# One ones matmul for two key blocks, whose exponentials GpSimd adds in place, in the attention stage of a three-stage kernel

## The reference

```
q, k, v = (heads(query), heads(key), heads(value))          # 16 heads, width 32
scores = jnp.einsum('bhqd,bhkd->bhqk', q, k)                 # 1024 x 1024, causal
at  = jax.nn.softmax(where(causal, scores, -inf) / sqrt(32), axis=-1)
out = jnp.einsum('bhqk,bhkd->bhqd', at, v) ... @ w_o + b_o
```

## Time and profile before

| | |
|---|---|
| median of 3 runs | 1262.74 us (1262.4 to 1263.25) |
| profiled execution | 1264.52 us, span 1262.7 us |
| busy, share of the span | PE 87%, DVE 72%, ACT 63%, POOL 29% |
| granted TensorE clock, mean | 0.956 |
| `core(0)` | about 457 to 626 us |
| out-projection, `project(1)` | about 626 to 658 us, 658 to 720 us |
| `core(1)` | about 722 to 894 us |

### The profile page before, as it was taken

How to read it: one execution, slowest core, us unless ns; L and a number is a source line. 1 busy time by engine, 2 the same in 40 slices (tenths; PEclk the granted TensorE clock), 3 DMA queues, 4 the chain that set the end, 5 groups by cost and what they waited for, 6 DMA issues and landing times. The chain is left out here.

```text
span 1262.7 us, 18129 instructions
## 1 busy us (share of the span) xinstructions
PE 1100.0 (87%) x5990; PEld 493.5 (39%) x5990; DVE 908.0 (72%) x2247; ACT 793.0 (63%) x1181; POOL 367.1 (29%) x400
## 2 busy tenths in 40 slices
PE   0777999987869789999999799999799799998886
PEld 0333555544434323232344233322244355554443
DVE  5788788988943787885334887783236888888793
ACT  5468798887623536667614356567235888988762
POOL 2101144444562144100220450002100124443356
PEclk9998899998998889999999899999899999999899
DMA  9200000000010222110000321110000000000000
GB/s 369 82 1 1 2 1 1 2 1 1 1 47 9 51 59 52 48 39 2 1 21 6 77 53 43 35 35 2 1 1 1 1 1 18 18 18 18 18 18 34
DMA packets 22286, 37.44 MB, mean 30 GB/s; under 512 B 5398, under 2 KB 7833, under 8 KB 21532
## 3 DMA queue, kind: packets, MB, share of 16 engines
q1 hardware_dynamic: 21404, 34.54, 8.6%
q0 software_dynamic: 768, 1.57, 0.5%
HBM read 19.17 MB, written 4.21 MB: 19 GB/s over the span
## 5 line engine op out<-in xcount | busy, mean ns | idle before, releaser
L802 ACT ACTIVATE arena<-arena,X 128x2048 int8<-128x2048 f32 x148 | 296.0, 2007 | 8.8 <-DVE X L1228 8.6
L857 ACT ACTIVATE arena<-zP,asc 128x512 f32<-128x512 f32 (+3 forms) x384 | 200.6, 582 | 109.3 <-PE zP L652 78.7
L502 PE MATMUL zP<-T,arena 128*128 128x512 f16 x1024 | 251.7, 390 | 6.7 <-DVE arena L1187 6.7
L554 PE MATMUL oP<-T,arena 128*128 128x512 f16 x832 | 206.2, 393 | 7.5 <-DVE arena L1343 7.5
L758 ACT ACTIVATE arena<-zP,sc 128x512 f32<-128x512 f32 x128 | 87.9, 689 | 107.7 <-PE zP L507 107.7
L502 PEld LDWEIGHTS zP<-T,arena 128*128 128x128 f16 x1024 | 102.5, 101 | 133.4 <-issue 16.7
L554 PEld LDWEIGHTS oP<-T,arena 128*128 128x128 f16 x832 | 83.2, 100 | 89.1 <-issue 18.7
L648 PE MATMUL zP<-arena 98*128 98x512 f16 (+3 forms) x384 | 110.6, 334 | 2.9 <-DMA arena<-arena 1.9
L1468 DVE RECIPROCAL arena<-arena 128x128 f32<-128x128 f32 x64 | 57.1, 927 | 61.7 <-ACT arena L870 61.7
L629 PE MATMUL hP<-arena 96*128 96x512 f16 (+3 forms) x256 | 84.4, 352 | 15.8 <-DVE mx L1446 12.9
L973 POOL TENSOR_SCALAR ln<-ln 128x1 f32<-128x1 f32 x32 | 38.6, 1206 | 202.5 <-DVE ln L1172 202.3
(11 more groups left out here) (196 smaller groups left out, 1876.1 us busy)
## 6 DMA issues: line engine op xcount, KB each, us to landing
arena<-arena SPq DMA_DIRECT2D x168, 64.0 KB, 2.0
arena<-in_w_synT SPq DMA_DIRECT2D x4, 1024.0 KB, 8.2
arena<-in_w_outT SPq DMA_DIRECT2D x4, 1024.0 KB, 14.8
out_dram<-x_sb SPq DMA_DIRECT2D x16, 256.0 KB, 2.0
x_sb<-in_x SPq DMA_DIRECT2D x3, 1024.0 KB, 14.0
arena<-in_w_o SPq DMA_DIRECT2D x2, 1024.0 KB, 5.0
arena<-arena POOLq DMA_DIRECT2D x24, 64.0 KB, 1.9
arena<-in_b_syn SPq DMA_DIRECT2D x1, 1024.0 KB, 11.9
```

Of the source, the lines that this page charges most:

```text
L502: pe.matmul(zP[:, c * CW:(c + 1) * CW], part[:, g % 2, k, :], T1[:, k, c * CW:(c + 1) * CW], start=(n == 0 and k == 0), stop=False)
L554: mm = pe.matmul(o, part[:, k, :], T2[:, k, :], start=(c == 0 and n == 0 and k == 0), stop=False)
L802: act.activation(junk[:, counted[0] % 2, :], Z[:, g % ZR, :], ACT.Sign, bias=X[:, 2, k:k + 1], accum_out=S[:, k:k + 1]).then_inc(sm["cnt"], 1)
L857: act.activation(PT[:, m // 4 % 2, h, q0:512], colP[m % 3][:, q0:512], ACT.Exp, scale=asc[:, g, 10:11]).then_inc(sm["exp_done"], 1)
```

## The change

In the pair of an odd key block kb and the even one before it, GpSimd adds the odd block's exponentials onto the even one's in memory, and PE then does one ones matmul for both, as wide as the even block. The product with v still reads each block. So:

- `core_order`: the ones matmul of blocks (kb-2, kb-3) stands at the end of step kb = 3, 5, 7, and that of a unit's last pair at the end of step 0 of the next unit. 48 ones matmuls of four heads in a batch become 24.
- Four buffers in place of two: `w_in` itself, the two of `PT`, and a part of `qk_mem` (from group 2 on, a part of `parts_mem`). ACT waits for the pair that used the buffer before.
- As `w_in` is overwritten, SP loads it again for batch 1, after the barrier and ahead of `w_lat`, and `project(1)` waits for it.
- POOL walks through the order too: `add_pair` at the last `col` of each odd block, the multiply and bias add of a unit at its last `rec`, and with each of the first four of these two tiles of the `bo` add.

The line numbers of the changed file are higher than before: ones matmul L693, `mix_v` L681, `col` L668 and L672, rows L649, turn L655, pair add L1059, multiply and bias add L1093 and L1094, `bo` add L1068, `w_in` loads L442.

```
             if last:
                 step.insert(len(step) - MIX_LAG, ("mix_v", *last))
-                step.append(("mix", *last))
+                if kb == 0:
+                    step.append(("mix", *last))
+                elif kb % 2 and kb >= 3:
+                    step.append(("mix", g, qc, kb - 2))
...
+        BLOCKS = [as_block(w_in.rearrange("p k n -> p (k n)")), PT[:, 0, :, :], PT[:, 1, :, :],
+                  as_block(qk_mem[:, 2048:4096]), as_block(parts_mem[:, HALF:HALF + 2048])]
+        def pt_of(g, kb):
+            return BLOCKS[4 if g >= 2 and kb % 4 == 3 else kb % 4]
...
             for b in range(2):
+                if b:
+                    eng.wait_ge(sm["mix_done"], b * TOTAL["mix"])
+                    load_w_in()
                 for k, w in ((0, w_ku), (1, w_qu), (2, w_qr), (3, w_vu)):
...
             def project(b):
-                pe.wait_ge(sm["aw_in"], 16 * 3 * KD)
+                pe.wait_ge(sm["aw_in"], 16 * 3 * KD * (b + 1))
...
+                    elif kind == "mix":
+                        qc, kb = e[2:]
+                        pe.wait_ge(sm["pair_set"], m + 1)
+                        if kb == 1 and n["norm"]:
                             pe.wait_ge(sm["sum_out"], n["norm"])
-                        q0 = max(0, kb * P - qc * 512)
+                        q0 = max(0, (kb - 1) * P - qc * 512)
                         for h in range(HG):
+                            mm = pe.matmul(sumP[h * HD:(h + 1) * HD, q0:512], ones32, pt_of(g, kb - 1)[:, h, q0:512],
+                                           start=(kb == 1), stop=(kb == 4 * qc + 3),
                                            tile_position=(0, h * HD), skip_group_check=True)
...
-                        if m // 4 >= 2:
-                            act.wait_ge(sm["mix_done"], m // 4 - 1)
+                        if m // 4 >= 4:
+                            act.wait_ge(sm["mix_done"], m // 8 - 1)
...
+                def add_pair(g, qc, kb, col):
+                    even, odd = pt_of(g, kb - 1), pt_of(g, kb)
+                    q0 = max(0, kb * P - qc * 512)
+                    pool.wait_ge(sm["exp_done"], col + 1)
+                    pool.wait_ge(sm["mv_done"], col // 4)
+                    pool.tensor_tensor(even[:, :, q0:512], even[:, :, q0:512], odd[:, :, q0:512], ALU.add)\
+                        .then_inc(sm["pair_set"], 1)
+                    pool.wait_ge(sm["pair_set"], col // 8 + 1)
...
+                for e in ORDER:
...
+                    if kind == "col" and e[3] % 2 and e[4] == HG - 1:
+                        add_pair(g, *e[2:4], m)
+                    elif kind == "norm" and m % TOTAL["norm"] == 0:
                         wait_stack(pool, b, 0)
                         wait_stack(pool, b, 1)
+                        units(2)
+                    elif kind == "rec" and e[3] == 3:
...
+                        pool.wait_ge(sm["mix_out"], b * TOTAL["norm"] + u + 1)
+                        pool.wait_ge(sm["rec_set"], m + 1)
+                        link(pool.tensor_tensor(a, a, rec_of(u), ALU.mult))
+                        pool.tensor_scalar(a, a, bcols[:, 10 + g:11 + g], None, ALU.add).then_inc(sm["attn_set"], 1)
+                        if u < 4:
+                            add_bo(range(2 * u, 2 * u + 2))
```

More of the change, by code:

```diff
@@ L263, in program @@
                  "h_set hT_ps hT_hi hT_lo mm2 out_ps y_set stats2 rstd2 yn_set x_new out_done "
[L264 removed]
+                 "consts2 mv_done pair_set bsyn_in hT_sub hT_lo2 ch_dve ch_act ch_pool phase "
                  "aw_in al_in ab_in a_stats a_rstd a_xn a_turn a_xT p_ps p_out p_max q_max q_scale split_hi split_lo wo_in bo_in "
@@ L424, in _, with load_w_in @@
                 eng.dma_start(brow[0:3, first:first + j * P], b_rows[:, first:first + j * P]).then_inc(sm["orow_in" if n else "brow_in"], 16)
+            def load_w_in():
+                for k in range(KD):
+                    for w, lo in ((w_kv, 0), (w_q, 128), (w_kr, 256)):
+                        eng.dma_start(w_in[:, k, lo:lo + w.shape[1]], w[k * P:(k + 1) * P, :]).then_inc(sm["aw_in"], 16)
             eng.wait_ge(sm["hT_ps"], 4 * NT)
-            for k in range(KD):
-                for w, lo in ((w_kv, 0), (w_q, 128), (w_kr, 256)):
-                    eng.dma_start(w_in[:, k, lo:lo + w.shape[1]], w[k * P:(k + 1) * P, :]).then_inc(sm["aw_in"], 16)
+            load_w_in()
             barrier(eng, 1)
             for b in range(2):
+                if b:
+                    eng.wait_ge(sm["mix_done"], b * TOTAL["mix"])
+                    load_w_in()
                 for k, w in ((0, w_ku), (1, w_qu), (2, w_qr), (3, w_vu)):
@@ L1018, in core, with units @@
             def core(b):
-                for g in range(3):
-                    if g == 1:
-                        load_stack(pool, b, 1, 1)
-                    elif g == 2:
+                def units(g):
+                    pool.memset(stacks[g][3 * HD:3 * HD + 2, 1, :, :], MUNIT).then_inc(sm["unit_set"], 1)
+                    pool.wait_ge(sm["unit_set"], 3 * b + g + 1)
+                def add_pair(g, qc, kb, col):
+                    even, odd = pt_of(g, kb - 1), pt_of(g, kb)
+                    q0 = max(0, kb * P - qc * 512)
+                    pool.wait_ge(sm["exp_done"], col + 1)
[3 more added lines that the diff above has]
+                    pool.wait_ge(sm["pair_set"], col // 8 + 1)
@@ new lines, in add_bo @@
+                def add_bo(tiles):
+                    pool.wait_ge(sm["bo_in"], 16 * (b + 1))
+                    pool.wait_ge(sm["a_xn"], (b + 1) * BT)
+                    for i in tiles:
+                        t = x_sb[:, b * BT + i, :]
+                        pool.tensor_tensor(t, t, bo, ALU.add).then_inc(sm["bo_added"], 1)
+                units(0)
+                load_stack(pool, b, 1, 1)
+                units(1)
+                n = {k: b * v for k, v in TOTAL.items()}
+                for e in ORDER:
+                    kind, g = e[:2]
+                    m = n[kind]
+                    n[kind] += 1
+                    if kind == "col" and e[3] % 2 and e[4] == HG - 1:
+                        add_pair(g, *e[2:4], m)
+                    elif kind == "norm" and m % TOTAL["norm"] == 0:
@@ L1024, in core @@
                         wait_stack(pool, b, 0)
                         wait_stack(pool, b, 1)
-                    pool.memset(stacks[g][3 * HD:3 * HD + 2, 1, :, :], MUNIT).then_inc(sm["unit_set"], 1)
-                    pool.wait_ge(sm["unit_set"], 3 * b + g + 1)
-                pool.wait_ge(sm["bo_in"], 16 * (b + 1))
-                pool.wait_ge(sm["a_xn"], (b + 1) * BT)
-                for i in range(BT):
-                    t = x_sb[:, b * BT + i, :]
-                    pool.tensor_tensor(t, t, bo, ALU.add).then_inc(sm["bo_added"], 1)
@@ L1033, in core @@
-                for m in range(TOTAL["norm"]):
-                    if b == 0 and m == TOTAL["norm"] - 1:
-                        rstd_rows(1, range(2))
-                    g, qc = m // 2, m % 2
-                    a = attT[:, g, qc * 512:(qc + 1) * 512]
-                    pool.wait_ge(sm["mix_out"], b * TOTAL["norm"] + m + 1)
-                    pool.wait_ge(sm["rec_set"], 4 * (b * TOTAL["norm"] + m + 1))
-                    link(pool.tensor_tensor(a, a, rec_of(m), ALU.mult))
-                    pool.tensor_scalar(a, a, bcols[:, 10 + g:11 + g], None, ALU.add).then_inc(sm["attn_set"], 1)
+                        units(2)
+                    elif kind == "rec" and e[3] == 3:
+                        u = m // 4 % TOTAL["norm"]
+                        if b == 0 and u == TOTAL["norm"] - 1:
+                            rstd_rows(1, range(2))
+                        qc = u % 2
+                        a = attT[:, g, qc * 512:(qc + 1) * 512]
+                        pool.wait_ge(sm["mix_out"], b * TOTAL["norm"] + u + 1)
[4 more added lines that the diff above has]
+                            add_bo(range(2 * u, 2 * u + 2))
```

22 lines of the change are left out of this document (13 added, 9 removed).

## The result

The changed kernel takes **1304.62 us** (1301.9 to 1306.24, four runs), the kernel before 1262.99 us beside it (1262.4 to 1265.44). The ratio is 1.0324, 95% interval 1.0299 to 1.0348. Forecast were 1290 us and slower, with a range of 1262 to 1312. The profiled execution took 1301.9 us, its span is 1300.1 us.

A forecast was written before the change was run, and what follows sets the result against it. PE, in its fixed order, was taken to bound the attention stage. 2 x (4.1 + 3 + 2) + 7.3 + 2.4 = +27.9 us made the profiled 1264.5 into 1292.4, the median about 1290; range 1262 to 1312.

The forecast's parts named there:

- PE's relief: Attention stage: odd blocks' ones matmuls fall away, 32 us less PE work, 16 a batch, an upper bound of the gain.
- The boundary: Ahead of project(1): the second load of w_in costs +7.3 us with nothing to hide it, half clock after it +2.4.
- The pair add: On GpSimd: 4.4 us for 2048 elements, 3.4 for 1536, 1.27 for 512; 5.05 kept for the range.
- VectorE held behind GpSimd: Small VectorE operations wait for long GpSimd instructions: 8 us, slack takes more than half, +3 us a batch (0 to 8).
- The chain: GpSimd's add, multiply, bias add, output adds, second add make PE wait: net +4.1 us a batch, +7.8 with 5.05 us adds.
- what was credited against the waits: Units of the core: savings of 0.7 us in u0, 3.0 in u1, 1.5 each in u3 and u5.
- The clock: PE in the cores: half clock after waits for GpSimd, about 1.7 us more each, +2 us a batch (0 to 8).
- PE's busy time: Sign in the profile after: PE busy about 32 us less.
- u0 and u7: First and last unit of a core: -0.7 us in u0, as rows bind it, and 0 in u7.
- a core not shorter: Sign in the profile after: core not shorter although PE is busy less; a core under 160 us would refute the prediction.
- a hold above 2 us: Sign: VectorE's small operations on the maxima, successors of L1455, L1459 and L1460, with maxima above 2 us.
- PE waited 8 us a batch for the pair adds: Sign: PE or its weight loads waiting for POOL at the pair add, 10 us or more a batch, most in units 2 and 4.

The follow-up runs named there:

- e1: The changed kernel with the second load of w_in issued before the barrier between the batches: 1299.33 us, ratio 1.0282 to the kernel before.
- e3: The kernel before plus the 48 adds on memory nobody reads, GpSimd's new order and the second load ahead of the barrier; PE never waits for adds: 1281.69 us, 1.0138.
- e11: e3 with the work on the maxima done by two tensor_reduce in place of four operations: 1255.16 us, ratio 0.9928 to the kernel before.
- e12: The kernel before with the work on the maxima done by two tensor_reduce, nothing else: 1256.02 us, ratio 0.9932.
- e10: The changed kernel with the work on the maxima done by two tensor_reduce in place of four operations: 1284.8 us, ratio 1.0154 to the kernel before.
- e7: The kernel before with each odd key block's ones matmul cut to one column, 0.5 added to the sums, no adds: 1256.98 us, ratio 0.9921.
- e13: e10 with e1's early load, each unit's multiply and bias add behind the next unit's second pair add, output adds behind the last: 1254.8 us, 0.9931.

## Why the prediction was right, and where it was not

The sign was right, and so was the shape: a fixed loss at the boundary, and cores that lose more than PE's relief gives. The time was 14.6 us above the forecast, inside a wide range: the cores grew by 16.3 and 15.5 us and not by 9.1, and two terms of the sum that were too small, by some 3 and 4.4 us a batch, are what is missing.

- **The boundary** was forecast at +9.7 us and measured +9.9 (7.3 and 2.6). e1 takes it away again: 8.4 us of the stretch from core to core.
- **The pair add** was forecast at 4.4, 3.4 and 1.27 us, and took 4.53, 3.44 and 1.27. The Trainium skill's 4497 ns (GPSIMD Engine Reference, section 3.1) was nearer than my 4.4 for 2048 elements, which my rows had bounded by 5.05.
- **VectorE held behind GpSimd** was forecast at +3 us a batch. e3 against e11 has 10.5 us for the holds and the two operations less, before against e12 has 2.5 for the two operations: about 8 us a batch from the adds, the end of the range that I gave. In the changed kernel itself, after against e10, it is 8.4, less the same 2.5: some 6. This is the first term that was mis-sized, by half. I had let "slack take more than half"; but behind these operations stands the turn, and PE stands at the turn in order. The Trainium skill's rule (SBUF — State Buffer, "Who interferes with whom") agrees with the rows of the operations on the maxima: held were tensor_scalar, cast, and the tensor_tensor with two inputs in SBUF, each until the GpSimd instruction ended, and never tensor_reduce (189 to 191 ns in e10, eight of sixteen under a pair add), which that section says never contends on this chip. I had used the rule to price the loss, and not seen that it also names the remedy.
- **The chain** was forecast with PE's relief taken off: +4.1 us a batch, and +2 for the clock. e10 against e12, where no hold is left, has +10.5 for both together. So this sum was 4.4 short, the second mis-sized term. The waits themselves were well placed. The prediction made PE 2.8 us late in u2 and u4 and 1.8 in u6; e10 shows 3.44, 2.81 and 1.7. By unit, in `core(0)` (from one last copy out of oP to the next; the last two rows hold the clock as well):

```
                   u0    u1    u2    u3    u4    u5    u6    u7    sum
prediction       -0.7  -1.1  +2.8  -1.5  +2.8   0.0  +1.8   0.0   +4.1
e10 - e12        -0.2  -0.3  +3.9  -0.7  +2.6  +0.4  +1.5  +3.4  +10.5
after - before   +3.1  +1.6  +4.1  -0.5  +4.3  +0.5  +1.8  +1.6  +16.3
```

One fault lies in what was credited against the waits: the sum has u0, u1, u3 and u5 gain 0.7, 3.0, 1.5 and 1.5 before waits, 6.7 us. In e7, with no GpSimd in the way, they gain 0.1, 1.1, 1.6 and 0.8, and about 12 us of matmuls less make the whole core only 2.7 us shorter. PE comes sooner to places where DVE's maxima or ScalarE's copy bind it, and waits there. The other is u7 (+3.4, and +2.2 in `core(1)`), where I counted nothing behind the second pair's matmul: in e10 that one ran at half clock (1.93 us for 1.06), and the last pair add was waited for as well (0.64). e13 shows the chain from the other side: the same adds in another order, and 12.7 us are back in `core(0)`, 8.0 in `core(1)`.
- **The clock** was forecast at +2 us a batch. I can't give it a price apart from the gaps, since every run that took gaps away moved both. Its size is seen in PE's busy time in `core(0)`: down by 2 us in after, and by 13.4 in e13, with the same matmuls. After a wait for a pair add of 1.6 us it fell in e1 and not in after, so part of it is chance.
- **u0 and u7**, which the sum put at -0.7 and 0, were 3.1 and 1.6 us longer in after. In u0 L1509 was held (0.87 us), PE waited 1.23 us at the turn for 0.87, and the ones matmul at 473.92 took 1.94 us; u0 of e3, with the same adds, had no hold and no loss. In u7 PE waited 2.8 us in sum for three pair adds.

Of the signs that the prediction named, four came: a core not shorter, a boundary gap of some 7 us with half clock behind it, the add's duration, and a hold above 2 us. Two did not. PE's busy time fell by 12 us in the whole span and by 5 in the two cores, not by 32, because the prediction counted matmuls and not the clock they would run at. And PE waited 8 us a batch for the pair adds, not 10, with nothing in u4: the holds had made it late already. A wait that is hidden by another shows only when the other is taken away.

Left open: what the clock costs apart from the gaps, and why it falls after a gap in one execution and not after the same gap in another. Open is also how much of e13's gain in the cores comes from the late multiply and how much from the output adds; no run separates them.

## What to carry to other kernels

Before work is moved to GpSimd, list VectorE's operations of the kinds that were held here (tensor_scalar, cast, tensor_tensor on two SBUF inputs) and ask who waits for each; where one stands ahead of the bounding engine, turn it into one that is not held, before anything else, and count a row of small ones as one hold for each when the long instruction is cut up. Price the relief of a "bounding" engine by leaving the work out of the kernel before, which is one run: here, with PE 87% busy, 24 us less of matmuls gave 8.5. And in a helper's fixed order, put what somebody waits for ahead of what nobody does.

## What the hardware showed that I had not expected

- A tiny VectorE operation (0.17 us) was held for 3.18 us of a 3.42 us GpSimd add; a tensor_reduce of the same size, multiplying a pair and writing f16, took 189 to 191 ns in all 16 cases, 8 of which began under a pair add.
- Cut into four, an add held three small operations one after the other (0.76, 0.92, 0.91 us), each to the end of its own piece.
- The same matmul of u7 after the same gap of PE (1.63 and 1.62 us) took 1.06 us in after and 1.93 in e1; in e7 a gap of 0.77 us was followed by half clock in `core(0)` and by the whole clock at the same place of `core(1)`.
- The kernel before gains 0.7% with its maxima as two tensor_reduce alone (e12). 6.0 of the 8.4 us between the two profiled executions lie in the cores, most of it as 0.4 us in each unit that has rows, and nothing more in the one unit of `core(0)` whose turn was held.
